# An edge-attention loop on one core: one-hot compares with two tensor inputs over eight edge columns, and a chunk's keys decoded one turn ahead

## The reference, cut to what matters

```python
h = (x_flat @ W_gat).reshape(M, HEADS, NUM_EXPERTS)          # M = 32768 tokens, 4 heads, 4 experts
e = leaky_relu(a_src[src] + a_dst[dst], 0.2)                  # 524288 edges and M self loops
e_max = segment_max(e, dst)
ee = exp(e - e_max[dst])
agg = segment_sum(h[src] * (ee / denom[dst])[:, :, None], dst)
# layer norm over agg, mean over heads, top 2 of 4 experts, softmax: a gate for each token
out = sum over experts of gate * (gelu(x @ W1[e] + b1[e]) @ W2[e] + b2[e])
```

## Time and profile before

| what | value |
|---|---|
| time, median of 3 runs | 10095.95 us (10090.94 to 10100.3) |
| span of the profiled execution, first to last instruction | 10069.6 us |
| DVE busy | 5609.3 us (56%) |
| POOL busy | 5042.1 us (50%) |
| PE busy | 4088.4 us (41%) |
| mean granted TensorE clock | 0.709 of full speed |

### The profile page before, as it was taken

One profiled execution on the slowest core, in us unless ns is written; L12 is line 12 of the kernel. 1 busy time (PEld: TensorE's weight loads), 2 busy tenths in 40 slices (PEclk: granted clock), 3 DMA queues, 4 the chain that ended last, 5 costly groups with the idle time before them and its releaser, 6 DMA issues. The chain is left out here.

```text
span 10069.6 us, 67922 instructions
## 1 busy us (share of the span) xinstructions
PE 4088.4 (41%) x14109; PEld 1997.0 (20%) x14171; DVE 5609.3 (56%) x16515; ACT 1868.9 (19%) x3239; POOL 5042.1 (50%) x4836
## 2 busy tenths in 40 slices
PE   0011388833344444434444444344444444334233
PEld 0010255521111111112111111111111121111100
DVE  9999788845444444444444444444444444444388
ACT  0000377721111111111111111111111111111111
POOL 0000155545566556665656556665666556665452
PEclk9855688866676777677776777667776777667655
DMA  0000133311111111111111111111111111111156
GB/s 17 0 0 0 55 120 118 120 46 31 31 44 32 31 31 36 39 32 31 32 43 32 31 31 35 40 32 31 31 44 32 31 31 35 40 32 27 44 191 199
DMA packets 351386, 467.68 MB, mean 46 GB/s; under 512 B 176559, under 2 KB 252290, under 8 KB 334338
## 3 DMA queue, kind: packets, MB, share of 16 engines
q1 hardware_dynamic: 203562, 408.25, 11.6%
q0 software_dynamic: 147552, 56.95, 5.9%
HBM read 234.91 MB, written 229.93 MB: 46 GB/s over the span
## 5 line engine op out<-in xcount | busy, mean ns | idle before, releaser
L739 POOL DMA_INDIRECT e_got<-rows,e_index x4352 | 4285.0, 985 | 2982.4 <-DVEq L800 1674.8
L751 PE MATMUL e_count_ps<-e_is_hi,e_is_lo 128*128 128x256 bf16 x4096 | 699.1, 328 | 3044.3 <-DMA keys<-s_u_b 2348.6
L879 DVE TENSOR_SCALAR e_is_lo<-e_iota_b,e_tlo 128x128 bf16<-128x128 bf16 x4096 | 1057.3, 258 | 1534.1 <-issue 1174.2
L880 DVE TENSOR_SCALAR e_is_hi<-e_iota_b,e_thi 128x256 bf16<-128x256 bf16 x4096 | 1184.2, 290 | 1247.4 <-issue 1247.2
L1332 ACT ACTIVATE ex_hh<-ex_hid_ps,ex_b 128x512 f32<-128x512 f32 x1024 | 696.7, 687 | 5889.8 <-remote 2776.9
L751 PEld LDWEIGHTS e_count_ps<-e_is_hi,e_is_lo 128*128 128x128 bf16 x4096 | 426.0, 114 | 3391.5 <-DMA keys<-s_u_b 2419.4
L1296 PE MATMUL ex_out_ps<-ex_hs,ex_w 128*128 128x512 f32 x1024 | 757.8, 832 | 18.1 <-remote 11.4
L1250 PE MATMUL ex_hid_ps<-ex_tn,ex_w 128*128 128x512 f32 x1024 | 661.3, 734 | 0.0
L1301 PE MATMUL ex_kept_ps<-ex_hh,ex_w 128*128 128x512 f32 x1024 | 542.1, 611 | 273.2 <-ACT ex_kept L1324 187.4
L864 DVE TENSOR_TENSOR e_wgt<-e_got,e_rp 128x1088 f32<-128x1088 f32 x64 | 180.5, 2820 | 681.1 <-issue 499.9
L180 POOL MEMSET m_identb<- 128x128 bf16 x1 | 0.2, 205 | 1077.7 <-POOLq L85 1077.7
(11 more groups left out here) (358 smaller groups left out, 6435.0 us busy)
## 6 DMA issues: line engine op xcount, KB each, us to landing
e_got<-rows,e_index POOLq DMA_INDIRECT x4352
kept<-ex_kept SPq DMA_DIRECT2D x64, 1024.0 KB
c_kept<-kept SPq DMA_DIRECT2D x64, 1024.0 KB
sums<-e_out SPq DMA_DIRECT2D x64, 816.0 KB
m_xin<-in_x_dram SPq DMA_DIRECT2D x64, 512.0 KB, 4.6
mid<-m_xm SPq DMA_DIRECT2D x64, 512.0 KB, 2.9
norm<-m_tn SPq DMA_DIRECT2D x64, 512.0 KB, 4.7
ex_tn<-norm SPq DMA_DIRECT2D x64, 256.0 KB
```

The costliest lines, as they stand in the source:

```text
L739: pool.indirect_dma_start(got[:, at % 2, c, :], None, rows_d, bass.IndirectOffsetOnAxis(ap=index[:, at % 2, c:c+1], axis=0)).then_inc(S["g ...
L751: last = pe.matmul(count_ps[:, 0:HIS], is_lo[:, g % 2, t, :], is_hi[:, g % 2, t, :], start=(isinstance(k, int) and k == 0 and g == 0 and t ...
L879: v.tensor_scalar(is_lo[:, g % 2, t, :], iota_b[:, 0:P], tlo[:, n:n+1], None, ALU.is_equal)
L880: last = v.tensor_scalar(is_hi[:, g % 2, t, :], iota_b[:, :], thi[:, n:n+1], None, ALU.is_equal)
```

## The change

Two edits in `attention`.

The first is in `one_hot`: instead of 16 `tensor_scalar` there are two `tensor_tensor` with both inputs broadcast, one over 8 columns x 128 (`is_lo`), one over 8 columns x 256 (`is_hi`). The digits `tlo` and `thi` become bf16, so that all operands have 16 bits. The digit's innermost step is zero (one element read 128 or 256 times).

The second: the decoding becomes a function `decode(k, at, turn)`. Chunk 0 is decoded before the loop, and body(k) on DVE begins with the decoding of chunk k+1. `index`, `start`, `cont` and `cut` get four buffers instead of two, and the wait for the gathers of chunk k-2 before `index` is gone. POOL's two waits stay as they were.

```diff
-        index = sb("index", [P, 2, COLS], I32); first = sb("first", [P, 1], I32)
-        start = sb("start", [P, 2, COLS]); cont = sb("cont", [P, 2, COLS]); cut = sb("cut", [P, 2, COLS])
+        index = sb("index", [P, 4, COLS], I32); first = sb("first", [P, 1], I32)
+        start = sb("start", [P, 4, COLS]); cont = sb("cont", [P, 4, COLS]); cut = sb("cut", [P, 4, COLS])
...
-        tlo = sb("tlo", [P, COUNT_TILES]); thi = sb("thi", [P, COUNT_TILES])
+        tlo = sb("tlo", [P, COUNT_TILES], BF16); thi = sb("thi", [P, COUNT_TILES], BF16)
...
+                decode(0, 0, 0)
                 def body(k, at, turn):
+                    if not isinstance(k, int) or k + 1 < CHUNKS:
+                        decode(k + 1, at + 1, turn)
                     if decodes(k):
                         u = at % 2
...
-                        if not isinstance(k, int) or k >= 2:
-                            v.wait_ge(S["gat%d" % ((at - 2) % 4)], 16 * COLS * ((at - 2) // 4 + 1) + 16 * COLS * turn)
...
-                        for t in range(RING):
-                            n = g * RING + t
-                            v.tensor_scalar(is_lo[:, g % 2, t, :], iota_b[:, 0:P], tlo[:, n:n+1], None, ALU.is_equal)
-                            last = v.tensor_scalar(is_hi[:, g % 2, t, :], iota_b[:, :], thi[:, n:n+1], None, ALU.is_equal)
+                        ring = slice(g * RING, (g + 1) * RING)
+                        for table, digit, width in ((is_lo, tlo, P), (is_hi, thi, HIS)):
+                            last = v.tensor_tensor(table[:, g % 2, :, :], iota_b[:, 0:width].unsqueeze(1).broadcast_to([P, RING, width]),
+                                                   digit[:, ring].unsqueeze(2).broadcast_to([P, RING, width]), ALU.is_equal)
                         last.then_inc(S["hot"], 1)
```

More of the change, by code:

```diff
@@ L778, in _, with decode, go @@
                 v.tensor_copy(iota_b[:, :], iota_i[:, :]).then_inc(S["iot"], 1)
+                def decode(k, at, turn):
+                    u, w = at % 2, at % 4
+                    i = [0]
+                    def go(ins):
+                        i[0] += 1
+                        ins.then_inc(S["dec"], 1)
+                        v.wait_ge(S["dec"], DEC * k + i[0])
+                    v.wait_ge(S["key%d" % u], 16 * (at // 2 + 1) + 32 * turn)
+                    kk = key[:, u, :]
+                    go(v.tensor_scalar(sgn[:, :], kk, 31, None, ALU.arith_shift_right))
+                    go(v.tensor_tensor(mag[:, :], kk, sgn[:, :], ALU.bitwise_xor))
+                    go(v.tensor_scalar(low[:, :], mag[:, :], 16, None, ALU.logical_shift_right))
+                    go(v.scalar_tensor_tensor(out=seg[:, :], in0=sgn[:, :], scalar=float(FLIP), in1=low[:, :], op0=ALU.mult, op1=ALU.add))
+                    go(v.tensor_scalar(dfull[:, :], seg[:, :], float(SHIFT + HALF * half), None, ALU.add))
+                    go(v.tensor_tensor(mag[:, :], mag[:, :], dfull[:, :], ALU.bitwise_xor))
+                    go(v.tensor_scalar(index[:, w, :], mag[:, 1:COLS+1], 65535, None, ALU.bitwise_and))
+                    v.sem_inc(S["idx"], 1)
+                    go(v.tensor_tensor(start[:, w, :], seg[:, 1:COLS+1], seg[:, 0:COLS], ALU.not_equal))
+                    go(v.tensor_scalar(cont[:, w, :], start[:, w, :], -1.0, 1.0, ALU.mult, ALU.add))
+                    go(v.tensor_scalar(cut[:, w, :], start[:, w, :], -BIG, None, ALU.mult))
+                    if isinstance(k, int) and k == 0:
+                        go(v.tensor_copy(prev_seg[:, :], seg[:, 0:1]))
+                        go(v.tensor_copy(first_seg[:, :], seg[:, 1:2]))
+                        v.tensor_scalar(first[:, :], dfull[:, 1:2], 65535, None, ALU.bitwise_and).then_inc(S["edge"], 1)
+                    else:
+                        go(v.tensor_copy(last_seg[:, :], seg[:, COLS:COLS+1]))
+                        go(v.tensor_copy(last_seg[:, :], seg[:, COLS:COLS+1]))
+                    assert i[0] == DEC
@@ L789, in body @@
[L789 to L794, removed]
@@ L802, in body @@
[L802 to L810, removed]
@@ L847, in body @@
                         by_head = lambda ap: ap.unsqueeze(1).broadcast_to([P, HEADS, COLS])
-                        go(v.tensor_tensor(adv[:, :, :], g[:, :, 20:24].rearrange("p c h -> p h c"), by_head(start[:, q, :]), ALU.mult)); settle()
+                        go(v.tensor_tensor(adv[:, :, :], g[:, :, 20:24].rearrange("p c h -> p h c"), by_head(start[:, w, :]), ALU.mult)); settle()
                         for h in range(HEADS):
-                            go(v.tensor_tensor_scan(ad[:, q, h, :], cont[:, q, :], adv[:, h, :], ad[:, 1 - q, h, COLS-1:COLS], ALU.mult, ALU.add))
+                            go(v.tensor_tensor_scan(ad[:, q, h, :], cont[:, w, :], adv[:, h, :], ad[:, 1 - q, h, COLS-1:COLS], ALU.mult, ALU.add))
                         settle()
@@ L866, in body @@
                         for h in range(HEADS):
-                            for w in range(EXPERTS + 1):
-                                ch = h * EXPERTS + w if w < EXPERTS else HEADS * EXPERTS + h
-                                data = wgt[:, h, w, :] if w < EXPERTS else rp[:, 1, h, :]
+                            for lane in range(EXPERTS + 1):
+                                ch = h * EXPERTS + lane if lane < EXPERTS else HEADS * EXPERTS + h
+                                data = wgt[:, h, lane, :] if lane < EXPERTS else rp[:, 1, h, :]
                                 go(v.tensor_tensor_scan(out[:, q, :, ch], rp[:, 0, h, :], data, out[:, 1 - q, COLS-1, ch:ch+1], ALU.mult, ALU.add))
```

19 lines of the change are left out of this document (4 added, 15 removed).

## The result

The changed kernel takes 10192.95 us (median of 4; the kernel before 10094.06 beside it): a ratio of 1.0086, 95% interval 1.0064 to 1.0108. It is 0.9% slower, where 9415 us was forecast.

A forecast was written before the change was run, and what follows sets the result against it. It took the bound to be each turn's slow stretch, where DVE issues one instruction per 1.40 us beside POOL's gathers. 98.4 + 4 = 102 us a turn against 113.3, over 60 turns, saves 680 us: 9415 us, range 8580 to 10100.

The forecast's parts named there:

- The durations of the compares: DVE's one-hots: low compare 1.22 us, high compare 2.28 us, a step with `ex_hs` 4.0 us.
- The slow stretch begins at 31, so nearly all of it is fast: One-hot phase after the attention: `ex_o`, eight steps x 4.0 us and two small copies, 0 to 33 us.
- the 63 us at 1.40 us an instruction behind it: From 33 to 95.9 us DVE does 45 instructions of decoding, digits and attention; nine scans left end at 98.4 us.
- In a slow stretch, then, DVE's time is its number of instructions x 1.40 us, and waits between them add little: Pricing rule for DVE: a one-hot step inside the slow stretch falls from 22.4 us to 4.2 us.
- Two-input compares and POOL: Compares with two inputs hold up POOL's gathers: 14 us a turn or nothing, taken as 4 us.
- The 11.0 us ahead of `e_wgt`: DVE's wait for the exponential in the attention, 11.0 us a turn, was to go.
- The gain goes to other waits: Rival: PE and ACT's `ex_kept` steps stretch, the exponential comes late; 110 to 117 us a turn, 10050 us; chance 0.20.
- The slow stretch never ends: Rival: gathers of two chunks stand close, DVE stays at 1.40 us an instruction; 124.6 us a turn, 10775 us; chance 0.14.
- The gathers bound the turn: Rival: DVE needs some 52 us, POOL's gathers never stop; 88.4 us a turn, 8600 us; chance 0.20.

The follow-up runs named there:

- e2: Changed kernel with the old one-input compares (`tensor_scalar`, f32 digits), so decoding one turn ahead alone; ratio 1.1470 to the kernel before.
- e7: Changed kernel with one product into `count_ps` a step in place of eight; ratio 0.9758 to the kernel before.
- e1: Kernel before with the new `one_hot` and bf16 digits, decoding in its old place; ratio 0.9908 to the kernel before.
- e5: Changed kernel with POOL waiting after every 17 gathers until those have landed; ratio 0.9678 to the kernel before.
- e17: Changed kernel with the old one-input compares and POOL waiting after every 9 gathers until they land; ratio 0.9408 to the kernel before, 9436 us.
- e9: Changed kernel with the old one-input compares and a one-column POOL memset ahead of every gather; ratio 1.1258 to the kernel before.

## Why the prediction was wrong, by its own steps

- **The durations of the compares, right.** 1216 and 2280 ns against 1.22 and 2.28 us. The rule that I cited from the Trainium skill (Vector Engine (DVE) Microarchitecture Reference, section 5.1), one element a cycle with the repeated 16-bit element, agrees with these rows: 1064 ns for the 1024 elements that the high compare has more. A fast step is 3.9 to 4.0 us, as forecast.
- **"The slow stretch begins at 31, so nearly all of it is fast", and the 63 us at 1.40 us an instruction behind it: the step that failed.** I took 31 us after the first gather as a property of the gathers. The runs show something that behaves as a backlog, filled by other engines' instructions too: in e2, with the one-hots right behind the first gather, it begins after some 12 us, and that half alone costs 14.7%. In the changed kernel 18 turns begin their one-hots with the chunk's first gather, as forecast, and all their steps are fast. But what I priced as slow then is not: decoding, digits and attention take 39 us (5168.84 to 5208.05), 18.59 of them waiting, where the sum has 65. So DVE's turn is over after 71 us, while the chunk that POOL gathers takes 118.7. The sum supposes that the two stay in step, and they do not: DVE runs ahead, waits for gathers later on, and comes to its one-hots in the midst of them. In 14 turns the one-hots begin 25 to 35 us after the first gather of a chunk that follows the one before by 0.3 us; there the eight `ex_hs` span 162 to 166 us, and the turn takes 198 us or more. Five others that begin 18 to 26 us after such a first gather have no long step. Why those stay fast is argued only: the two-input compares space the gathers out before the backlog is there.
- **"In a slow stretch, then, DVE's time is its number of instructions x 1.40 us, and waits between them add little", false.** 18 instructions took 155 us. What comes late there is PE's signals, the later the more PE instructions stand ahead (e7, an estimated 0.8 to 1.35 us each). They were as late before (32.9 us between two `ex_hh`, 32.2 after), so a step in the slow stretch could not become 4 us. Its mean rose from 17.4 to 27.4 us; both means hold steps that lie in the stretch in part, so their difference is no price.
- **Two-input compares and POOL: right in kind, mis-sized.** I took 4 us a turn, 14 at most, "near the low end, since POOL's delay only counts where it moves that end". The mean chunk takes 12.5 us more (99.9 for 87.4), a chunk with two one-hot phases 31 us more. The new compares do it: e1, where they stand alone, has 97.7 us a chunk, and e2, without them, 84.7. The time counts, since the attention waits for the gathers, 42 us in the turn shown. The Trainium skill (SBUF — State Buffer, Who interferes with whom) has it that a DVE instruction with two SBUF inputs holds up GpSimd's reads. The gathers of 1.44 to 3.96 us agree; that rule has nothing on the long steps of PE and ACT.
- **The 11.0 us ahead of `e_wgt`.** They did not go: 591.6 us of idle time in all, for 681.1 before, and 18.59 us in the turn shown.
- **The rivals.** "The gain goes to other waits" was the one that came true in outline: steps of PE and ACT stretched in the slow stretch, but the one-hot steps and not those of `ex_kept` that I named (these only in e7), and I put it at 10050. "The slow stretch never ends" is not the changed kernel, but it is nearly e2, at 11506 us. "The gathers bound the turn" is what e5 and e17 reached, at 104 to 109 us a turn and not 88.4.

What stays open is what the backlog is made of. Gathers and the instructions of PE and DVE take part in it, and POOL standing still until its transfers have landed clears it. No view of the profile names it. Every time here comes with a span and a granted clock, so it is the time of a recorded execution, and whether the recording of each instruction has a part in the backlog no run shows.

## What to carry to other kernels

When a stretch is slow on an engine, look at what every other engine does in it, and at how late each one's signals come, before you price it by the slow engine's own instructions; a cut there may leave another engine's lateness as it was. And look at single turns beside the mean: here a mean of 115.6 us was made of turns of 63 to 204 us. Long runs of indirect DMAs from POOL can slow engines that have nothing to do with them: count how many follow each other, and try a wait for their landing after every few (9 of 68 here, worth 6%) before you rebuild the work beside them. Run the halves of a change apart: here they were worth -0.9% and +14.7%.

## What I had not expected of the hardware

- Standing still can pay: seven waits in each chunk's gathers, 16.5 us more of POOL's time per chunk (103.9 for 87.4), made the program 6% faster.
- PE, which reads nothing that is gathered, is slowed beside the gathers: its signal arrives 17 to 27 us after its product, and its instructions between two signals cost an estimated 0.8 to 1.35 us each. ACT's signal to DVE arrived at once in one step shown and 3.4 us late in the other.
- The pace of 1.40 us is no fixed price: after a wait of 21 us sixteen compares ran in 2.7 us in the same stretch (e2).
- Two-input compares of 2.28 us hold a gather up to 3.96 us, and a memset of 0.12 us between gathers costs POOL nothing outside a slow stretch (e9, starts 1.25 us apart).
